# Cross-attention on one core: V in ten tiles of another cut, eight of them among the row maxima, and the program's two blocks joined

## The reference

```python
Q = split_heads(query @ Wq + bq)
K = split_heads(key @ Wk + bk)          # key = value = context, 77 tokens
V = split_heads(value @ Wv + bv)
scores = jnp.einsum('bhqd,bhkd->bhqk', Q, K) / np.sqrt(D_K)
attn = jax.nn.softmax(scores, axis=-1)
ctx = jnp.einsum('bhqk,bhkd->bhqd', attn, V)
out = ctx.transpose(0, 2, 1, 3).reshape(B, S, D_MODEL) @ Wo + bo
return _layer_norm(out + query, ln_gamma, ln_beta)
```

## Time and profile before

| | |
|---|---|
| median of 3 runs | 623.35 us (622.33 to 623.76) |
| the profiled execution | 622.21 us |
| its span, first to last instruction | 620.4 us |
| mean granted TensorE clock | 0.995 |
| PE busy | 594.8 us (96%) |
| DVE, POOL, ACT busy | 496.9, 443.7, 362.9 us |
| chain that ended last | 87% PE |

### The profile page before, as it was taken

The page is one execution under the profiler, slowest core; times in us unless marked ns, Lnnn a source line. Parts: engine busy times, 40 slices in busy tenths (PEclk is TensorE's granted clock), DMA queues, the critical chain, the costliest instruction groups (busy, mean ns, idle before and its releaser), DMA issues.

```text
span 620.4 us, 12034 instructions
## 1 busy us (share of the span) xinstructions
PE 594.8 (96%) x3336; PEld 430.5 (69%) x3336; DVE 496.9 (80%) x913; ACT 362.9 (58%) x674; POOL 443.7 (72%) x395
## 2 busy tenths in 40 slices
PE   5998999999999999999999999999999999999992
PEld 5986765677777777777777777777777777777562
DVE  5423468888888888888888888888888888898776
ACT  5621235566666666666666666666666666655562
POOL 1335024648888888888888888888888888888785
PEclk9999999999999999999999999999999999999997
DMA  8859878988979898989898987979897989796523
GB/s 306 308 224 185 205 181 224 206 189 193 235 192 232 212 215 214 224 203 219 201 229 205 221 226 193 235 201 227 207 219 205 211 218 231 196 221 168 168 76 128
DMA packets 93392, 129.58 MB, mean 209 GB/s; under 512 B 49936, under 2 KB 49936, under 8 KB 93360
## 3 DMA queue, kind: packets, MB, share of 16 engines
q1 hardware_dynamic: 74352, 94.42, 60.8%
q10 hardware_dynamic: 19008, 34.78, 21.8%
HBM read 53.94 MB, written 24.35 MB: 126 GB/s over the span
## 4 chain that ended last, share of the span: by engine, by line
PE 87%; DVE 3%; issue 1%; ACT 1%; DVEq 0%; ACTq 0%
PE p_q L586 29%; PE p_o L652 27%; PE p_s L616 10%; PE p_v L627 10%; PE p_a L602 6%; PE p_o L99 3%; DVE nm L933 1%; PE p_a L669 1%; PE p_den L635 1%; DVE rden L898 0%; PE p_q L669 0%; ACT prob L721 0%; DVE part L888 0%; PE p_s L669 0%; ACT qh L736 0%
## 5 line engine op out<-in xcount | busy, mean ns | idle before, releaser
L721 ACT ACTIVATE prob<-p_s 77x512 f32<-77x512 f32 x256 | 143.2, 591 | 103.3 <-PE p_s L616 93.0
L1069 POOL TENSOR_TENSOR cl<-cxt,ch 128x512 fp32r<-128x512 f32 x64 | 83.1, 1299 | 110.0 <-ACT ch L746 110.0
L933 DVE TENSOR_REDUCE nm<-p_a 128x4 f32<-128x308 f32 x256 | 115.9, 475 | 49.1 <-PE p_a L602 48.0
L888 DVE TRANSPOSE_TENSOR_REDUCE part<-prob 96x64 f32<-96x2048 f32 x64 | 146.4, 2287 | 1.6 <-issue 1.3
L736 ACT ACTIVATE qh<-p_q,bq_col 128x512 fp32r<-128x512 f32 x64 | 44.0, 687 | 124.6 <-PE p_q L586 124.6
L586 PE MATMUL p_q<-xh,wqh 128*128 128x512 f32 x256 | 101.1, 395 | 1.7 <-PEq L151 1.7
L586 PE MATMUL p_q<-xl,wqh 128*128 128x512 f32 x256 | 101.2, 395 | 0.0
L586 PE MATMUL p_q<-xh,wql 128*128 128x512 f32 x256 | 101.0, 394 | 0.0
L616 PE MATMUL p_s<-z,ks 97*77 97x512 f32 x256 | 95.6, 413 | 2.4 <-ACT prob L721 2.4
L652 PE MATMUL p_o<-woh,ch 128*128 128x512 f32 x240 | 95.4, 398 | 0.8 <-issue 0.7
L652 PE MATMUL p_o<-wol,ch 128*128 128x512 f32 x240 | 94.6, 394 | 0.0
(11 more groups left out here) (128 smaller groups left out, 930.1 us busy)
## 6 DMA issues: line engine op xcount, KB each, us to landing
z<-qh SPq DMA_DIRECT2D x256, 128.0 KB, 3.8
z<-ql SPq DMA_DIRECT2D x124, 128.0 KB, 4.8
xn<-in_x ACTq DMA_DIRECT2D x60, 256.0 KB, 3.3
out_dram<-y SPq DMA_DIRECT2D x60, 256.0 KB, 4.3
xt<-in_x_t ACTq DMA_DIRECT2D x58, 256.0 KB, 5.0
ks<-k_high SPq DMA_DIRECT2D x32, 154.0 KB, 4.8
cx<-in_ctx_t SPq DMA_DIRECT2D x4, 616.0 KB, 6.0
k_high<-kth SPq DMA_DIRECT2D x4, 616.0 KB, 3.6
```

Of the source, the lines that this page charges most:

```text
L721: nc.scalar.activation(prob[0:S2, j, :], p_s[j % 2][0:S2, :], ACT.Exp, scale=SCALE).then_inc(prob_ready, 1)
L888: nc.vector.tensor_reduce(part[:], prob[0:KP, :, :].rearrange("p h (i r) -> p (h i) r", r=DK), AX_X, ALU.add, apply_transpose=True).then_i ...
L933: nc.vector.tensor_reduce(nm[:, t, g.k % 2:HALF:2], p_a[t % 2][:, 0:HC * S2].rearrange("p (h k) -> p h k", k=S2), AX_X, ALU.max, negate=Tr ...
L1069: nc.gpsimd.tensor_tensor(cl[:, i, g.k % NCH, :], cx[:, g.k % 2, :], ch[:, i, g.k % NCH, :].bitcast(F32), ALU.subtract).then_inc(cl_ready, 1)
```

## The change

- V_FIRST = 2: the opening makes two V tiles, of 128 and 80 tokens. The eight others are all of 128 tokens, one in each of slots 0 to 7, their 12 products in triples ahead of the four p_a, where p_o's triples stand from slot 8 on. DVE adds bv at the start of the next slot and ACT stores the tile there.
- N1 is now 208: cx1 holds 208 tokens, cx2 1,024, laid out by V tile and depth; K's three tiles have 208, 512 and 512 columns.
- wvh and wvl have memory of their own. Wo is split in slots 1 and 3, all four chunks through xn; load_wo(2) and (3) wait for the first two to be split and stand in SP's slot 2. The loads of gamma, beta and bo go from slot 6 to slot 5.
- The divided context has one buffer instead of two: `divide(g)` waits for ch and cl of group g-1 instead of g-2. Two unused tensors go, and the memory for descriptors made in software is set to 2,048.
- Both blocks are one: no barrier. ACT, DVE, POOL and SP wait for `context_done` (K stored, Wq split, two V tiles out) instead; PE for `k_low_out`, `wq_low` and, ahead of the first p_a, `v_out`. SP loads kb0 and two chunks of x ahead of V's stores.

```diff
-WO_SLOTS = (6, 7)
-
-V_FIRST = 4
-V_SLOTS = (0, 1, 2, 3, 4, 5)
+WO_SLOTS = (1, 3)
+ROWS_SLOT = 5
+
+V_FIRST = 2
+V_LATE = 8
...
-    return [(r, min(P, B * S2 - r)) for r in range(0, B * S2, P)]
...
+    late = B * S2 - V_LATE * P
+    assert P < late <= V_FIRST * P
+    return [(0, P), (P, late - P)] + [(late + P * k, P) for k in range(V_LATE)]
+
+
+def v_row(i):
+
+    return (i + V_FIRST) % 4
+
+
+def v_stores(tiles, row):
+
+    return 16 * len([i for i in tiles if v_row(i) == row])
+
+
+def v_products(nc, keep, bank, cxh, cxl, kc, m):
+
+    wvh, wvl = keep["wvh"], keep["wvl"]
+    for n, (x, w) in enumerate(((cxh, wvh), (cxh, wvl), (cxl, wvh))):
+        last = nc.tensor.matmul(bank[0:m, :], x, w[:, kc, :],
+                                start=(kc == 0 and n == 0), stop=(kc == KC - 1 and n == 2))
     return last
...
-    N1 = V_FIRST * P
-    cuts = [0, N1, N1 + (NK - N1) // 4 * 2, NK]
+    N1 = NK - V_LATE * P
+    cuts = [0, N1, (N1 + NK) // 2, NK]
...
-            return [V_FIRST + n for n, k in enumerate(V_SLOTS[:VT - V_FIRST]) if k == PAIR * g.u + g.k]
+            return [V_FIRST + n for n in range(V_LATE) if n == PAIR * g.u + g.k]
...
-        block = ctx.enter_context(nc.Block())
+        def context_done(engine):
+
+            for i in range(2):
+                engine.wait_ge(k_stored[i], 16 * KC)
+            engine.wait_ge(wq_low, KC)
+            engine.wait_ge(v_out, V_FIRST)
...
-                if g.back(WO_SLOTS[0] - 1).is_first():
+                if g.back(WO_SLOTS[0] + 1).is_first():
                     load_wo(2)
                     load_wo(3)
...
+                    if g.is_first():
+                        pe.wait_ge(wq_low, KC)
+                        pe.wait_ge(k_low_out, 3 * KC)
...
+                    if g.is_first():
+                        pe.wait_ge(v_out, V_FIRST)
...
-            def project_v(i):
-
-                pe.wait_ge(v_out, i)
-                r, n = tiles_v[i]
-                v_products(nc, keep, p_vp[:], keep["cx2"], r - V_FIRST * P, n).then_inc(v_summed, 1)
+            def project_v(i, kc):
+
+                if kc == 0:
+                    pe.wait_ge(v_out, i)
+                m = tiles_v[i][1]
+                cxh, cxl = (t[:, i - V_FIRST, kc, :] for t in keep["cx2"])
+                last = v_products(nc, keep, p_o, cxh, cxl, kc, m)
+                if kc == KC - 1:
+                    last.then_inc(v_summed, 1)
...
-                for i in v_in_slot(g):
-                    project_v(i)
...
                         project_out(o, kc)
+                    for i in v_in_slot(g):
+                        project_v(i, kc)
...
-                at_least(dve, ch_ready, g.over(1, -1))
-                at_least(dve, cl_ready, g.over(1, -1))
-                nc.vector.tensor_tensor(cx[:, i, :], p_v[:], rden[:], ALU.mult).then_inc(cx_ready, 1)
+                at_least(dve, ch_ready, g.over(1))
+                at_least(dve, cl_ready, g.over(1))
+                nc.vector.tensor_tensor(cx[:], p_v[:], rden[:], ALU.mult).then_inc(cx_ready, 1)
...
+                for i in v_in_slot(g.back(1)):
+                    add_bv(i)
...
-                        if t == 1:
-                            for i in v_in_slot(g):
-                                add_bv(i)
```

More of the change, by code:

```diff
@@ L114, in project_context @@
     xt, xh, xl, y, wvh, wvl, bv_row = (keep[n] for n in ("xt", "xh", "xl", "y", "wvh", "wvl", "bv_row"))
[L115 to L116 removed]
+    xt_in, xh_ready, xl_ready, v_stored, v_summed, v_out, k_stored, k_low_out, wq_low = (
+        keep[n] for n in ("xt_in", "xh_ready", "xl_ready", "v_stored", "v_summed", "v_out",
+                          "k_stored", "k_low_out", "wq_low"))
     with ExitStack() as ctx:
@@ new lines, in _, with high, k_high, x_high @@
+        @block.scalar
+        def _(act):
+            def high(part, signal):
+                raw, hi, _ = part
+                nc.scalar.copy(hi, raw).then_inc(signal, 1)
+            def k_high(i):
+                c, lo, hi = tiles_k[i]
+                act.wait_ge(k_summed, i + 1)
+                if c >= 2:
+                    act.wait_ge(k_stored[c % 2], 32)
+                nc.scalar.activation(kth[:, c % 2, lo:hi], pk[i % PK][:, 0:hi - lo], ACT.Identity,
+                                     bias=bk_col[:, c:c + 1]).then_inc(k_high_out, 1)
+            def x_high(n):
+                act.wait_ge(xt_in[n % 2], 16 * (n // 2 + 1))
+                nc.scalar.copy(xh[:, 0, n, :], xt[:, n % 2, :]).then_inc(xh_ready, 1)
+            for kc in range(KC):
+                act.wait_ge(wk_in[kc], 16)
+                high(first[3 * kc], kv_high)
+                act.wait_ge(cx_in[kc], 16)
+                high(first[3 * kc + 1], kv_high)
+                high(first[3 * kc + 2], kv_high)
+            act.wait_ge(biases_in, 32)
+            for i in range(PK):
+                k_high(i)
+            act.wait_ge(wv_in, 16)
+            for kc in range(KC):
+                high(first[3 * KC + kc], kv_high)
+            x_high(0)
+            x_high(1)
+            act.wait_ge(wq_in, 16)
+            for i in range(PK, 2 * PK):
+                k_high(i)
+                if i - PK < KC:
+                    high(second[i - PK], wq_high)
+            x_high(2)
+            x_high(3)
@@ new lines, in _, with x_low @@
+        @block.gpsimd
+        def _(pool):
+            nc.gpsimd.memset(keep["kb0"][:].bitcast(F32), 0.0).then_inc(keep["kb0_zeroed"], 1)
+            nc.gpsimd.memset(keep["minus_half"][:], -0.5)
+            sel = keep["sel"]
+            nc.gpsimd.memset(sel[:], 0.0).then_inc(sel_ready, 1)
+            for b in range(KP // DK):
+                pool.wait_ge(sel_ready, b + 1)
+                nc.gpsimd.affine_select(out=sel[:], in_=sel[:], compare_op=ALU.not_equal, fill=1.0, base=-DK * b,
+                                        pattern=[[-1, DK]], channel_multiplier=1).then_inc(sel_ready, 1)
+            def x_low(n):
+                pool.wait_ge(xh_ready, n + 1)
+                nc.gpsimd.tensor_tensor(xl[:, 0, n, :], xt[:, n % 2, :], xh[:, 0, n, :].bitcast(F32),
+                                        ALU.subtract).then_inc(xl_ready, 1)
+            x_low(0)
+            x_low(1)
+            for i, (raw, hi, lo) in enumerate(second):
+                pool.wait_ge(wq_high, i + 1)
+                nc.gpsimd.tensor_tensor(lo, raw, hi.bitcast(F32), ALU.subtract).then_inc(wq_low, 1)
+            x_low(2)
+            x_low(3)
@@ L337, in attend @@
     ch, cl = keep["ch"], keep["cl"]
-    xt_in, xh_ready, xl_ready, v_stored, v_summed, v_out = (
-        keep[n] for n in ("xt_in", "xh_ready", "xl_ready", "v_stored", "v_summed", "v_out"))
+    xt_in, xh_ready, xl_ready, v_stored, v_summed, v_out, k_stored, k_low_out, wq_low = (
+        keep[n] for n in ("xt_in", "xh_ready", "xl_ready", "v_stored", "v_summed", "v_out",
+                          "k_stored", "k_low_out", "wq_low"))
     tiles_v = v_tiles(B, S2)
     VT = len(tiles_v)
-    assert VT <= V_FIRST + len(V_SLOTS) and max(V_SLOTS) < LAG_PV + 2
     xt_dram = a["x_t"].rearrange("b (c p) s -> (b c) p s", p=P)
```

347 lines of the change are left out of this document (146 added, 201 removed).

## The result

| | before | after |
|---|---|---|
| median | 623.52 us (622.33 to 624.89, 14 runs) | 620.52 us (14 runs; 13 of them from 615.61 to 622.50) |
| ratio of after to before | | 0.9943, 95% interval 0.9922 to 0.9964 |
| the profiled execution | 622.21 us | 621.88 us |
| its span, mean clock | 620.4 us, 0.995 | 620.1 us, 0.989 |

By the medians the kernel is 3.0 us faster (by the ratio 3.5, interval 2.2 to 4.9); 8.7 were forecast (614.7, range 612.3 to 619.5), so the sign was right and the size was not. One execution of after, 731.97 us at a clock of 0.753, was disturbed and is left out of the ratio. The 13 others are not alike: 615.61 had a mean clock of 0.995, 617.11 and 617.17 had 0.991 and 0.992, and the ten from 620.0 up had 0.989 to 0.991. The profiled one is of the ten.

What follows compares the result with a forecast made beforehand. TensorE, busy 96% of the span, was taken as the bound. Terms -1.9 - 5.6 + 0.8 + 1.0 - 2.1 - 0.9 = -8.7 us gave 613.5 profiled, 614.7 beside the runs' median; range 612.3 to 619.5.

Steps and rivals of the forecast that it cites:

- 1, the join: Between opening and slot 0: PE no longer waits at the barrier and restarts; 1.9 us gained.
- Rival C: The gap at the join stays (branch, instruction fetch or late semaphore); 1.9 us not gained, 616.6; chance 0.08 together with D.
- 2, V out of the opening: Opening: two V tiles, 24 products at 0.233 us, leave; 5.6 us gained there, paid back in the slots.
- 3, the narrow products: K products of the opening, now 208+512+512 columns: 0.115 us per 208-column product; 0.8 us lost, ends 0.0 and 4.4.
- Rival B: The opening's 208-column K products run at unrounded f32 pace, 0.36 us each; 11.8 us more, 626.5; chance 0.12.
- 4, the first tile: Start of the opening: PE waits for the wider context split, and its clock may rise later; 1.0 us lost, ends 0.3 and 1.5.
- 5, slots 0 to 7: Slots 0 to 7 take 60.95 us instead of 63.1, a gain of 2.1 although 24 more products are in them.
- 12.8 us: SP's chain of 16 z loads, second qh to landing, kept its old length; PE then waits 0.5 us in slot 3.
- Rival A: Late loads (z, kb0, ks) in the first slots, sharing SP's queue and DMA engines; 3 us more, 617.7; chance 0.18.
- no change: Whole kernel: a measurement within about 0.2%, 1.25 us, of before; chance 0.04.
- 6, slot 8: Slot 8: PE's first Wo product no longer waits for POOL's last wol; 0.9 us gained.
- 7, one buffer: Each slot: DVE's divide waits for POOL's subtraction of the slot before, with 3.7 us to spare; cost nothing.

Runs made afterwards that it cites:

- two-block kernel: The changed kernel with the barrier put back (two blocks again), all else the same; 619.76 us, ratio 0.9944 to before.
- Wo later: The changed kernel with Wo's loads moved to slots 3 and 5 and split in slots 4 and 6; 617.10 us, ratio 0.9922 to before.
- kb1 later: The changed kernel with the four loads of kb1 moved behind z's first loads in SP's queue; 618.10 us, ratio 0.9922 to before.
- V ahead: The changed kernel with slot 3's 12 V products ahead of its first scores instead of between the maxima; 616.31 us, ratio 0.9882 to before.
- filled slot 3: The changed kernel with 16 extra unread products in slot 3 ahead of the first scores; 618.38 us, ratio 0.9909 to before.
- the best kernel: The changed kernel with Wo loaded in the opening, split after x, nine V products ahead in slot 3, 15 unread early products; 614.82 us, ratio 0.9871 to before.

## Why the prediction was right in sign and wrong in size

By the medians -8.7 was forecast and -3.0 measured. The parts can be read only in the profiled executions, where -0.3 was measured: that of before lies 1.3 below its median, that of after 1.4 above its own. So the account below explains a miss of 8.4, of which 2.7 belong to the executions that were profiled. By its own parts:

**1, the join: right.** V's last product starts at 42.36, p_q at 42.59, the stream's own step. 1.84 gained on PE, as forecast; the two-block kernel shows that it bought nothing in the end while z was late. Rival C is out.

**2, V out of the opening: right.** 24 products from 37.05 to 42.59, 5.5.

**3, the narrow products: right.** Forecast step 0.115, measured 0.11 (PE's timeline, after); with it the sum is 48 x (0.112 + 0.466 - 0.563) = 0.7. (The recorded sum of 0.8 should have read 0.9: 48 x 0.018.)

```profile
24.01 0.27 PE L309 MATMUL pk<-cx1h,wkh 128*128 128x208 f32 x1
24.12 0.27 PE L309 MATMUL pk<-cx1l,wkh 128*128 128x208 f32 x1
24.23 0.27 PE L309 MATMUL pk<-cx1h,wkl 128*128 128x208 f32 x1
```

From 23.67 to 24.68 there are nine steps, 0.112 each. Rival B (0.36) is out. The Trainium skill, page "TensorE: Matmul & The Clock Gate", section "LDWEIGHTS (loading the stationary operand)", gives 107 ns for a load of 128 columns; 0.112 us sits 5 ns above that and well above the 89 ns that the isolated gap of the section "Back-to-back issue gap" would give, which fits the weight load as the pace, as the prediction took it.

**4, the first tile: mechanism right, size just over its range.** Forecast 1.0, ends 0.3 and 1.5. K was through at 37.05 instead of 34.77, 2.28 later, of which the widths are 0.7: 1.6. The splits came as worked out (context cast 1.04, subtraction 1.23, done at 7.46) and PE waited 0.83 for it (rows of DVE and PE, for the earlier trace rows):

```profile
6.23 1.23 DVE L247 TENSOR_TENSOR cl<-cx,ch 128x1024 fp32r<-128x1024 f32 x1 [0.57 <-ACT ch L206]
...
7.51 0.80 PE L309 MATMUL pk<-ch,wkh 128*128 128x512 f32 x1 [0.83 <-DVE cl L247]
...
12.16 0.57 PE L309 MATMUL pk<-ch,wkh 128*128 128x512 f32 x1
12.57 0.39 PE L309 MATMUL pk<-cl,wkh 128*128 128x512 f32 x1
12.80 0.39 PE L309 MATMUL pk<-ch,wkl 128*128 128x512 f32 x1
```

What was mis-sized is the "some tenths" for a later rise of the clock: the steps of 0.43 end at 12.57, where the slow steps of before ended near 9.6. In kernels with the same opening they ended by 10.7 (Wo later, kb1 later), at 12.2 (two blocks) and at 13.0 or later (V ahead, filled slot 3), and K was through between 36.05 and 37.70. So this term is 0.6 to 2.2, by the execution.

**5, slots 0 to 7: the step that failed.** A gain of 2.1 was forecast and 5.8 lost (63.08 to 68.85): 7.9 of the 8.4 us missing; part 4 is the other 0.5. Slots 1 (6.48) and 4 to 7 (8.26 to 8.29) came as forecast, so the triples between the maxima work. What failed is the term "12.8 us" for z's chain, carried over unchanged from before. It is no constant: it holds 16 loads and the wait for the last to land, and the change put 512 KB of Wo, issued at 47.27, and x and kb1 nearer to it. It took 17.2, and began 0.9 after its qh: from the second qh to the scores 18.1 us, where the prediction had 12.35. The window shows the crowd (DMA rows of after, 50 to 56 us: packets, then issues with KB and us to landing):

```profile
DMA packets 2258, 1.30 MB, mean 217 GB/s; under 512 B 1901, under 2 KB 1901, under 8 KB 2257
...
xt<-in_x_t ACTq DMA_DIRECT2D x1, 256.0 KB, 8.7
ks<-k_high SPq DMA_DIRECT2D x1, 154.0 KB, 9.8
kb<-k_high SPq DMA_DIRECT2D x4, 38.5 KB, 6.4
```

SP's and ACT's queues took 102% and 18% of the 16 engines' time there, and only 217 GB/s moved; in the opening the same engines moved far more at a lower share (14 to 16 us: 403 GB/s at 1.04, here 1.22). One thing that differs is the size of the pieces: 1,901 of 2,258 are under 512 B, in the opening 10 of 404. The Trainium skill, page "DMA: Bandwidth & Descriptors", section "Specifications", asks for 512 B and more for full rate; the 217 against 403 GB/s agree with that. Moving such loads (kb1 later) and large ones (Wo later) both shortened the chain.

*Rival A* was this mechanism, with 0.18 and a price of 3 us. It was sized by "the spare of before gone twice", 0.5 and 3; PE waited 0.49 and 4.25, and 1.70 for qh, a path that the prediction didn't have: ACT issues and splits x in one order with qh, and a late x holds qh back. A also had no term for the clock that falls after a long wait, 3.05. With those it would have been, for the profiled execution, 613.5 + 5.74 (the waits, less the 0.7 already in the sum) + 3.05, some 622.3 (measured 621.88), and "no change" would have had a chance worth naming instead of 0.04.

**6, slot 8: right.** 8.29 (111.44 to 119.73), 0.9 less than before; POOL's wol is out of the way.

**7, one buffer: right.** DVE's divide still begins 3.7 us after cl's end (for the earlier trace rows), and the slots of the loop keep their pace, 8.29 in both kernels.

```profile
302.37 1.30 POOL L1104 TENSOR_TENSOR cl<-cxt,ch 128x512 fp32r<-128x512 f32 x1 [1.32 <-ACT ch L778]
...
307.37 0.69 DVE L953 TENSOR_TENSOR cxt<-p_v,rden 128x512 f32<-128x512 f32 x1
```

That the sign was right owes something to luck: in the profiled executions 6.1 us were gained (5.22 and 0.90) and 5.8 lost in slots 0 to 7, and nothing in the prediction kept the loss under the gain. And the forecast was not out of reach: one execution of after took 615.61, and "Wo later" takes Wo's loads out of slots 1 to 3 and has 617.10. What stays open: why the same kernel takes 615.6 once and 620.5 mostly (its mean clock of 0.995, that of before, suggests that it was without a long half-clock stretch; only the profiled execution can be looked into), and what share of K's slow last store in the best kernel is Wo's.

## What to carry to other kernels

When work is moved or taken out, the transfers around it come nearer together too: do not carry a chain of loads over with its old length, but count again what shares its queue and its engines, up to the last small load that somebody waits for. Where a wait of a few microseconds is left on TensorE, price the clock after it as well, here up to 3 us, and put work that is due anyway ahead of the wait. An edit whose gain shows on its own rows can still be worth nothing while a later chain sets the end (the barrier), so fix that chain first.
